# A stage run five tiles ahead instead of three, its lead taken back at two steps, with filling and draining written out by hand

## The reference, cut to what matters

```python
# x: 4096 tokens x 512
y   = x @ (W + delta_W).T                      # the second output of the layer isn't used
x1  = layernorm(x + y)                         # no scale, no shift
z   = x1 @ ternary(W_syn).T + b_syn            # 4096 x 2048
thr = top_k(z, 204)[0][:, -1:]                 # per token
h   = where(z >= thr, relu(z), 0)
o   = h @ ternary(W_out).T + b_out             # 4096 x 512
f   = layernorm(x1 + o) * gamma + beta
out = layernorm(x1 + f)                        # no scale, no shift
```

## Time and profile before

| | |
|---|---|
| median of 3 runs | 633.76 us |
| the profiled execution, its own time | 634.05 us |
| its span, from the first to the last instruction | 632.3 us |
| PE busy | 586.0 us (93%) |
| ACT busy | 544.0 us (86%) |
| DVE busy | 539.4 us (85%) |
| POOL busy | 376.3 us (60%) |
| mean granted TensorE clock | 0.976 of full |

### The profile page before, as it was taken

The page is one execution under the profiler, slowest core; times in us unless marked ns, Lnnn a source line. Parts: engine busy times, 40 slices in busy tenths (PEclk is TensorE's granted clock), DMA queues, the critical chain, the costliest instruction groups (busy, mean ns, idle before and its releaser), DMA issues.

```text
span 632.3 us, 8712 instructions
## 1 busy us (share of the span) xinstructions
PE 586.0 (93%) x2482; PEld 266.3 (42%) x2482; DVE 539.4 (85%) x657; ACT 544.0 (86%) x724; POOL 376.3 (60%) x712
## 2 busy tenths in 40 slices
PE   8799669999999999999999999999999999997573
PEld 7434324444444444444444444444444444443221
DVE  5796998998998899888888888898998888899882
ACT  1797659999999999999999999999999999989942
POOL 0126386777776547585565457545857555757773
PEclk9999789999999999999999999999999999999887
DMA  8982234545465454555454554545564454434462
GB/s 331 320 263 51 50 83 85 116 91 129 100 109 126 66 118 87 113 101 133 95 124 100 103 117 73 123 78 125 102 133 90 95 101 100 79 74 83 91 95 80
DMA packets 184581, 71.66 MB, mean 113 GB/s; under 512 B 168144, under 2 KB 176336, under 8 KB 183888
## 3 DMA queue, kind: packets, MB, share of 16 engines
q1 hardware_dynamic: 184528, 71.07, 51.2%
HBM read 20.72 MB, written 8.39 MB: 46 GB/s over the span
## 4 chain that ended last, share of the span: by engine, by line
PE 71%; DVE 8%; issue 6%; POOL 6%; ACT 3%; DMA 1%; DVEq 0%; POOLq 0%; ACTq 0%
PE z_ps L972 27%; PE o_ps L992 15%; PE u_ps L955 14%; PE o_ps L985 14%; ACT junk L542 2%; DVE w_sb L772 1%; DVE w_sb L815 1%; DVE z_sb L801 1%; POOL tmp L423 1%; DVE m L777 1%; POOL nmean L374 1%; POOL b L388 1%; ACT hh L579 1%; DVE hT L751 1%; POOL rs L384 1%
## 5 line engine op out<-in xcount | busy, mean ns | idle before, releaser
L542 ACT ACTIVATE junk<-z_sb,t_col 128x2048 f16<-128x2048 f32 x128 | 255.1, 1995 | 10.8 <-POOL t_col L442 9.8
L972 PE MATMUL z_ps<-t_syn,xhT 128*128 128x512 f16 x1024 | 231.0, 379 | 2.7 <-DVE t_syn L663 2.7
L972 PEld LDWEIGHTS z_ps<-t_syn,xhT 128*128 128x128 f16 x1024 | 99.8, 98 | 134.3 <-issue 18.1
L985 PE MATMUL o_ps<-t_out,hT 128*128 128x512 f16 x512 | 122.4, 395 | 16.8 <-DMA hT<-hh 12.4
L955 PE MATMUL u_ps<-weff,xT_sb 128*128 128x512 f32 x256 | 117.5, 602 | 2.3 <-ACT x1s L561 2.3
L992 PE MATMUL o_ps<-t_out,hT 128*128 128x512 f16 x512 | 116.1, 380 | 0.0
L423 POOL TENSOR_SCALAR tmp<-signs,dev 128x1 f32<-128x1 f32 x64 | 40.3, 629 | 124.3 <-ACT junk L542 123.4
L801 DVE SCALAR_TENSOR_TENSOR z_sb<-z_ps,sc,bias_z 128x1024 f32<-128x1024 f32 x64 | 82.0, 1280 | 18.4 <-PE z_ps L972 18.2
L772 DVE SCALAR_TENSOR_TENSOR w_sb<-z_sb,t_col 128x2048 f32<-128x2048 f32 x32 | 86.6, 2707 | 6.4 <-POOL t_col L442 6.2
L542 ACT ACTIVATE junk<-z_sb,start 128x2048 f16<-128x2048 f32 x32 | 64.0, 2001 | 29.7 <-DVE z_sb L801 29.7
L985 PEld LDWEIGHTS o_ps<-t_out,hT 128*128 128x128 f16 x512 | 51.5, 101 | 83.1 <-issue 16.0
(11 more groups left out here) (118 smaller groups left out, 605.4 us busy)
## 6 DMA issues: line engine op xcount, KB each, us to landing
xT_sb<-in_xT SPq DMA_DIRECT2D x16, 512.0 KB, 4.0
out_y<-y_sb SPq DMA_DIRECT2D x32, 256.0 KB, 2.9
z_sb<-in_w_synT SPq DMA_DIRECT2D x4, 1024.0 KB, 12.3
hh<-in_w_outT SPq DMA_DIRECT2D x2, 1024.0 KB, 9.6
z_sb<-in_w_outT SPq DMA_DIRECT2D x2, 1024.0 KB, 10.5
hT<-hh SPq DMA_TRANSPOSE x66, 4.3
weff<-in_wT SPq DMA_DIRECT2D x2, 512.0 KB, 4.7
w_sb<-in_dwT SPq DMA_DIRECT2D x2, 512.0 KB, 5.6
```

The costliest lines, as they stand in the source:

```text
L542: a_.activation(junk[:, n % 2, :], z_sb[:, t % ZS, :], ACT.Sign, bias=at, scale=-1.0, accum_out=signs[:, j, r:r + 1]).then_inc(counted, 1)
L972: last = mm(z_ps[:, c, b * BANK:(b + 1) * BANK], xhT[:, j, h * KD + k, :], t_syn[:, k, n0:n0 + BANK], start=k == 0 and h == 0, stop=k == K ...
L985: mm(o_ps[t % OS][:, :], hT[:, j, 0, c, :], t_out[:, c, :], start=c == 0, stop=False)
```

## The change

The constants `A_LN1` and `A_MM1` go from 3 to 5: in step s PE now makes mm1 of tile s + 5, and ACT square1 and ln1_out of it. hi_x stays at tile s + 3 (`A_HI`), lo_x and transpose_x at s + 1. `x1s` gets 10 buffers instead of 8. In steps 12 and 20 (`SKIPS`) mm1, square1 and ln1_out are left out, so that the lead is 4 tiles after step 12 and again 3 after step 20; `first_of(s)` gives the tile. The loop body serves steps 5 to 27 only, and is otherwise the one of before; steps 0 to 4 and 28 to 35 are written out on every engine. `COUNTS` lists ACT's counts in their order, for `count_no`. No tile's operations are added to or dropped; POOL makes 41 scales(s) instead of 39, since the first is now that of step -5.

```diff
 L_SEL, L_MM3, L_LN2, L_OUT = 2, 3, 4, 4
-A_X, A_LN1, A_MM1 = 1, 3, 3
+SKIPS = (12, 20)
+A_X, A_HI, A_LN1, A_MM1 = 1, 3, 5, 5
...
-ZS, XS, OS = 6, 8, 3
+ZS, XS, OS = 6, 10, 3
...
+def first_of(s):
+
+    return s + A_LN1 - sum(s >= k for k in SKIPS)
...
             transpose_x(0)
-            sp.dma_start(bias_z[:, :], b_syn.rearrange("(a n) -> a n", a=1).broadcast_to([P, N]))\
-                .then_inc(bsyn_loaded, 16)
-            load(1)
             load_out(0)
             load_out(1)
-            load_out(2)
-            transpose_x(1)
-            load_out(3)
+            load(1)
+            load(2)
             for k, src in enumerate((b_out, gamma, beta)):
                 sp.dma_start(vecs[:, k, :], src.rearrange("(a n) -> a n", a=1).broadcast_to([P, D])).then_inc(vec_loaded, 16)
-            load(2)
...
+            sp.dma_start(bias_z[:, :], b_syn.rearrange("(a n) -> a n", a=1).broadcast_to([P, N])).then_inc(bsyn_loaded, 16)
+            transpose_x(1)
+            load_out(2)
+            load_out(3)
+            load(3)
...
+            transpose_hi(29)
+            store(25)
+            transpose_lo(29)
+            store(26)
+            transpose_lo(30)
+            transpose_hi(30)
+            transpose_hi(31)
+            transpose_lo(31)
+            store(27)
...
             def scales(s):
-                j, a, l, e = s % 2, s + A_LN1, s - L_MM3, s - L_OUT
+                j, a, l, e = s % 2, first_of(s), s - L_MM3, s - L_OUT
...
+            update(0, 2)
+            update(0, 3)
+            second_base(1)
             scales(-1)
...
+            scales(0)
+            update(1, 2)
+            scales(1)
+            update(1, 3)
+            second_base(2)
...
+            count(1, 2)
+            ln1_out(-1, 4)
+            square1(0, 5)
+            ln1_out(0, 5)
+            hi_h(0)
+            square1(1, 6)
+            count(1, 3)
+            ln1_out(1, 6)
+            count(2, 0)
...
+            for s in range(FILLED, DRAIN):
+                count(s, 0)
+                square2(s, s - L_MM3)
+                if s not in SKIPS:
+                    square1(s, first_of(s))
...
+            for s in range(FILLED, DRAIN):
+                mm2(s, 0)
+                mm3_hi(s - L_MM3)
+                flags(s - L_SEL)
+                mm3_lo(s - L_MM3)
+                mm2(s, 1)
+                if s not in SKIPS:
+                    mm1(first_of(s))
```

More of the change, by code:

```diff
@@ new lines, in _ @@
+            scales(4)
+            update(4, 2)
+            mean_v(1)
+            add_beta(2)
+            update(4, 3)
+            for s in range(FILLED, DRAIN):
+                second_base(s)
+                mean_r(s - L_MM3)
+                add_bout(s - L_MM3 + 1)
+                scales(s)
+                update(s, 2)
+                update(s, 3)
+                mean_v(s - L_MM3)
+                add_beta(s - L_MM3 + 1)
+            second_base(28)
+            mean_r(25)
+            add_bout(26)
@@ new lines, in _ @@
+            count(2, 2)
+            ln1_out(2, 7)
+            hi_h(1)
+            count(2, 3)
+            hi_x(5)
+            square1(3, 8)
+            count(3, 0)
+            first_step(3)
+            count(2, 4)
+            square2(3, 0)
+            count(3, 1)
+            second_step(3)
+            count(3, 2)
+            ln1_out(3, 8)
+            hi_h(2)
+            count(3, 3)
+            square3(4, 0)
+            hi_x(6)
+            count(4, 0)
+            first_step(4)
@@ new lines, in _ @@
+            count(28, 0)
+            square2(28, 25)
+            first_step(28)
+            count(27, 4)
+            count(28, 1)
+            square1(28, 31)
+            second_step(28)
+            count(28, 2)
+            ln3_out(28, 24)
+            hi_h(27)
+            count(28, 3)
+            ln1_out(28, 31)
+            hi_x(31)
+            square3(29, 25)
+            count(29, 0)
+            first_step(29)
+            square2(29, 26)
+            count(28, 4)
+            count(29, 1)
@@ L881, in _ @@
             syn_scale()
-            for i in range(3):
-                syn_weights(i)
+            syn_weights(0)
+            syn_weights(1)
+            syn_weights(2)
             spread()
@@ L915, in _ @@
             out_weights(3)
[L917 to L942 removed]
+            evac(3, 0)
@@ new lines, in _ @@
+            below(26)
+            top8(26)
+            lo_x(29)
+            select(26)
+            centre(24)
+            hidden(26)
+            general(26)
+            add_v(28, 24)
+            evac(28, 0)
+            lo_h(26)
+            evac(28, 1)
+            add_r(25)
+            below(27)
+            top8(27)
+            lo_x(30)
+            select(27)
+            centre(25)
+            hidden(27)
+            general(27)
+            add_v(29, 25)
+            evac(29, 0)
@@ new lines, in _ @@
+            lo_h(27)
+            evac(29, 1)
+            add_r(26)
+            below(28)
+            top8(28)
+            lo_x(31)
+            select(28)
+            centre(26)
+            hidden(28)
+            general(28)
+            add_v(30, 26)
+            evac(30, 0)
+            lo_h(28)
+            evac(30, 1)
+            add_r(27)
+            below(29)
+            top8(29)
+            select(29)
+            centre(27)
+            hidden(29)
+            general(29)
+            add_v(31, 27)
@@ new lines, in _ @@
+            evac(31, 0)
+            lo_h(29)
+            evac(31, 1)
+            add_r(28)
+            below(30)
+            top8(30)
+            select(30)
+            centre(28)
+            hidden(30)
+            general(30)
+            add_v(32, 28)
+            lo_h(30)
+            add_r(29)
+            below(31)
+            top8(31)
+            select(31)
+            centre(29)
+            hidden(31)
+            general(31)
+            add_v(33, 29)
+            lo_h(31)
```

428 lines of the change are left out of this document (296 added, 132 removed).

## The result

| | before | after |
|---|---|---|
| median, side by side on one chip (7 runs each) | 633.43 us | 638.47 us |
| profiled execution, own time | 634.05 us | 637.83 us |
| its span | 632.3 us | 636.0 us |
| PE busy | 586.0 us | 582.7 us |
| mean granted clock | 0.976 | 0.982 |

PE works 3.3 us less at a slightly better clock, and the end still comes later. Where the time went is read by setting one operation of every step, mm3_lo, beside itself in the two traces.

What follows compares the result with a forecast made beforehand. PE was taken to bound the steady steps at 17.47 us, with DVE close behind. From 634.05 us, -6.9 (skips), +0.6 (filling), +0.3 (loads) and 0 (draining) gave 628.05, less 0.29: 627.8 us; 8-in-10 range 624.6 to 631.2 us.

Steps and rivals of the forecast that it cites:

- the catching up: Steps behind each skip: DVE bounds at 16.72 to 16.84 us a step until the lead is used up, 5.4 steps at most.
- Each takes 3.43 us off PE: Steady steps: each of the two skipped mm1 takes 3.43 us off PE, 6.9 us off in sum.
- 0.63 to 0.75 us: Steady steps: how far PE is ahead of DVE as the bound, taken as the gain of each step behind a skip.
- The clock in the skipped steps stays at 1.00: Stretches behind steps 12 and 20: granted clock stays at 1.00; the rival that it falls had 0.06, 632.7 us.
- The filling, +0.6: Filling: two more mm1 go in PE's gaps, and PE comes out about 0.6 us later, two tiles ahead.
- I take nothing for: Filling: count(1, 3), and update(1, 3) with it, move by some 5 us, priced at nothing.
- signs of being wrong: Steps of 17.2 or more with PE waiting, clock under 1, mm2 of tile 4 later than 102 us, evac(0, 0) awaiting bias_z.
- bias_z, +0.3: Loads in the filling: bias_z lands at 34.4 to 37.7 us, costing 0 to 1.7 us, taken as 0.3.
- The draining, 0: Draining: the new orders sum to 0, with -1.7 and +1.7 us as ends.
- the pair of tile 30: Draining: transpose_lo(30) ahead of transpose_hi(30) starts mm3_hi(30) at about 605; some 1.7 us lost, 1.7 won back at mm3_hi(31).
- short operations off no chain: Draining: the other new orders move short operations off no chain that the prediction could see, taken as 0.
- a dear filling: Rival, chance 0.08: in the filling mm1(5) to mm1(7) form one PE-ACT chain at half clock, 13.8 us more, 641.6 us.

Runs made afterwards that it cites:

- all_orders: The change with bias_z's load first, load(4) and transpose_x(5) issued earlier, and the draining in the steady order on all engines: 631.04 us, ratio 0.9966 to the kernel before.
- skips_12_13: all_orders with steps 12 and 13 skipped instead of 12 and 20: 633.72 us, ratio 0.9997 to the kernel before.
- a_load4: The change with load(4) issued between transpose_x(3) and transpose_hi(0) instead of behind transpose_x(4): 636.87 us, ratio 1.0046 to the kernel before.
- a_x5: The change with transpose_x(5) issued ahead of transpose_hi(2): 637.07 us, ratio 1.0056 to the kernel before.
- a_bias: The change with the load of bias_z put back right behind transpose_x(0), ahead of load_out(0): 637.29 us, ratio 1.0055 to the kernel before.
- skip_16: all_orders with only step 16 skipped, and a lead of four from then on: 631.89 us, ratio 0.9987 to the kernel before.
- best: all_orders with DVE's lo_x behind select from step 5 on, and steps 16 and 24 skipped instead of 12 and 20: 630.11 us, ratio 0.9932 to the kernel before.

## Why the prediction was wrong, point by point

By the two traces the sum's terms were these: the skips -6.9 forecast, -3.7 measured; filling and loads +0.9 forecast, +4.45 measured; the draining 0 forecast, +3.0 measured (1.87 + 1.1). Of the miss of 9.7 us in the span the skips are 3.2, the filling and the draining 6.5. With the skips alone mis-sized the time would have been 631.0 us, just inside the stated range, and all_orders did measure 631.04 (beside 633.72). So two steps failed: the catching up had the mechanism wrong, and the transfers that the new orders made late were left out of the sum or taken at nothing, and they turned a gain into a loss.

- **"Each takes 3.43 us off PE", the others following over five steps: the mechanism that failed.** It treated DVE's lag as a debt that could be worked off. For that PE would have to run ahead of DVE and stay ahead, and it can't: flags(s-2), in the middle of PE's row, needs ok of the same step. PE waits there at once (1.76 and 1.26 us), and waited time is gone. The 0.63 to 0.75 us that the prediction read is DVE's lead per step; what counts at a skip is how far ok has come ahead of flags by then. In the next step the mm1 is back, so a gain of 0.63 to 0.75 us a step has nothing to come from; PE's own 17.47 us are the longer. What a skip is worth is mm1's time less that wait: 1.60 and 2.10. Forecast 6.9, measured 3.7. The trace of before could have told it. In its step 13 ok ends at 262.32, 1.63 us ahead of flags, in step 21 at 401.59, 2.14 ahead, nearly what the two skips gave. Timeline of DVE, then of PE there, and PE's wait in the first step behind one without a mm1:

```profile
262.10 0.22 DVE L788 SCALAR_TENSOR_TENSOR ok<-m,t_col,hit 128x1 f32<-128x1 f32 x1
...
401.37 0.22 DVE L788 SCALAR_TENSOR_TENSOR ok<-m,t_col,hit 128x1 f32<-128x1 f32 x1
```

```profile
263.95 0.19 PE L1001 MATMUL z_ps<-ok,ones 128*1 128x1 f32 x2
...
403.73 0.19 PE L1001 MATMUL z_ps<-ok,ones 128*1 128x1 f32 x2
...
559.12 0.19 PE L1001 MATMUL z_ps<-ok,ones 128*1 128x1 f32 x2 [1.50 <-DVE ok L788]
```

  The last row is the same thing in the draining: 15.61 us from 543.63 to the next mm3_lo, 1.86 gained at once, with 1.50 of wait.
- **The clock in the skipped steps stays at 1.00**: right. Windows of the kernel after:

```profile
256.00:266.00 10.00, 9.04 (x42) 3.92 (x40) 9.36 (x7) 8.96 (x14) 7.37 (x14) 1.00 0.80 182
...
396.00:406.00 10.00, 8.74 (x43) 3.85 (x42) 9.58 (x13) 8.89 (x12) 6.04 (x13) 1.00 0.69 157
```

  skips_12_13 showed a case in which it falls.
- **The filling, +0.6**: the walk through mm1(5) (66.9 forecast, 66.35 seen), mm1(6) (75.1; 74.59) and flags(1) (92.6; 93.72) was near. "I take nothing for" update(1, 3) was wrong: below(1) waits 1.04 us for it and begins at 87.87 instead of 86.35 (the rest DVE was late already). The larger miss is that the walk ended at flags(1) and followed PE alone: load(4) and transpose_x(5), moved on SP's queue, were not priced. Their waits are 1.73 and 1.24 us, and a_load4 and a_x5 put them at 2.0 and 1.4 us. Two of the prediction's own signs of being wrong came from here and from bias_z: the first mm2 of tile 4 begins at 102.74, later than 102, and evac(0, 0) waits. (The mm1 at 95.64 "from which it is never short of work" was a small misreading: before, too, PE waits 0.56 us at flags at 124.17.)
- **bias_z, +0.3**: it landed past the slow end of the two bandwidths (evac at 37.83 against 34.4 to 37.7), 1.8 us late; a_bias gave 1.5, not clear of its noise. The same reordering also moved load(1), which wasn't looked at.
- **The draining, 0**: the mechanism of the pair of tile 30 was right, loss and winning back both, but the loss was 4.9 us instead of the 3.7 taken (605 - 601.28), and about 1.1 stayed. hi of tile 30 was to go out about 4 us later; it goes out at 604.00 instead of 596.27, and 2.3 of these 7.7 us PE was late already. Missed was transpose_lo(26) ahead of transpose_x(29), 1.87 us, written off as one of the "short operations off no chain"; it stands in the orders as plainly as the other.
- **The range** (624.6 to 631.2) took a dear filling only as the chain between PE and ACT, 10 us at once. Five small transfers in one queue, some 1 to 2 us each, were a way to the same side that it had no price for.

## What to carry to other kernels

Taking work off the busiest engine in one step gains only the slack of the next engine in that step: read the wait that will take its place, and space such steps so that the slack can grow again (0.6 us a step here, so three or four steps by the rows; only distances of one and of eight steps were run). In a queue that issues strictly in order, list each transfer that the new order puts another in front of, and give each the time by which its reader will miss it. When an order written out by hand replaces a rule, each pair that differs deserves a run of its own, since a gain of 3 us and four losses of 1.4 to 2.1 us look like one bad idea.

## What the runs showed of the hardware that was not expected

- below (DVE) took 3.39 us in step 12 and 2.35 us in step 16 of skip_16, for the same shape. In the first GpSimd's add_beta runs beside it in its usual time; in the second it is add_beta that is stretched. Timeline of POOL in the kernel after, and in skip_16 (where below began at 325.69):

```profile
260.02 1.26 POOL L450 TENSOR_TENSOR x1g<-x1s,vecs 128x512 f32<-128x512 f32 x1
```

```profile
325.87 3.30 POOL L434 TENSOR_TENSOR x1g<-x1s,vecs 128x512 f32<-128x512 f32 x1
```

  One of the two engines is held up, DVE by 1.0 us or GpSimd by 2.0. In the first pair add_beta begins 0.02 us ahead of below, in the second 0.18 us behind it; in best's step 16 it begins 0.03 us behind and below is held up all the same (3.45 us). At step 20 add_beta begins 0.52 us ahead (397.69) and below takes 2.89. That would explain why a skip was worth 1.6 us at step 12, 2.1 at step 20 and 2.3 at step 16. This was read from the traces only, and no run moved add_beta to prove it.
- Identical instructions split at 33.4 us into executions 3 us apart, through a wait of under 1 us and a mm1 of 3.70, 5.40 or 6.76 us. In the draining a wait of 1.84 us stood ahead of an mm3_lo of 3.63 us in the kernel before (575.07) and of one of 5.31 in the kernel after (577.06), while every mm3_lo behind the steady steps' waits of 1.04 to 1.81 us took its 3.63. What tells these apart was not settled.
